# A four-layer block on one core, two lanes woven by tables of beats: one shared table per engine becomes one per lane

## The reference

```
x = x + jnp.tanh(g_xattn[0]) * _L0_xattn_ref(_layernorm(x, axis=-1), ctx_1024, ...)   # 16 heads of 8
x = x + jnp.tanh(g_ffn[0])   * _L0_ffn_ref(_layernorm(x, axis=-1), ...)    # 8 experts, top 2, plus shared
x = x + jnp.tanh(g_xattn[1]) * _L1_xattn_ref(...)                          # 16 heads of 8, biases
x = x + jnp.tanh(g_ffn[1])   * _L1_ffn_ref(...)    # self-attention, values and outputs by 8 experts a head
x = x + jnp.tanh(g_xattn[2]) * _L2_xattn_ref(...)                          # mLSTM, 4 heads
x = x + jnp.tanh(g_ffn[2])   * _L2_ffn_ref(...)                            # quantised, with a convolution
x = x + jnp.tanh(g_xattn[3]) * _L3_xattn_ref(...)                          # one wide head and an MLP
x = x + jnp.tanh(g_ffn[3])   * _L3_ffn_ref(...)                            # 16 experts, top 4, plus shared
```

```
v = jnp.einsum('bthe,bted->bhtd', mix_v, proj_v)
...
attn = jnp.einsum('bhij,bhjd->bihd', probs, v)
...
res = jnp.einsum('bthe,bthd,efd->bthf', mask_o, attn, Wo)
```

## Time and profile before

| | before |
|---|---|
| median of 3 runs (lowest to highest) | 2517.3 us (2514.52 to 2517.75) |
| the profiled execution's own time | 2514.25 us |
| its span, first to last instruction | 2512.2 us |
| busy: PE, DVE, ACT | 87%, 70%, 51% of the span |
| mean granted TensorE clock | 0.98 of full |
| DMA | 115.45 MB, mean 46 GB/s |

### The profile page before, as it was taken

One profiled execution on the slowest core, in us unless ns is written; L12 is line 12 of the kernel. 1 busy time (PEld: TensorE's weight loads), 2 busy tenths in 40 slices (PEclk: granted clock), 3 DMA queues, 4 the chain that ended last, 5 costly groups with the idle time before them and its releaser, 6 DMA issues.

```text
span 2512.2 us, 50619 instructions
## 1 busy us (share of the span) xinstructions
PE 2196.2 (87%) x19506; PEld 1569.4 (62%) x19506; DVE 1748.2 (70%) x5567; ACT 1282.0 (51%) x3714; POOL 141.0 (6%) x180
## 2 busy tenths in 40 slices
PE   7998889988899888998889988899888998899887
PEld 3667556675567755676556765557655576555765
DVE  6864777757777477774877757777487775777657
ACT  4365354654446544474444734447344473444734
POOL 0000100001000010000000011000110001100010
PEclk9999999999999999999999989999899998999999
DMA  4034000330004300042000520005100051000510
GB/s 168 1 92 96 17 5 1 99 88 18 5 1 105 82 17 5 1 117 70 18 5 1 134 53 20 3 1 139 48 20 3 1 139 48 20 3 8 145 35 5
DMA packets 312512, 115.45 MB, mean 46 GB/s; under 512 B 268752, under 2 KB 295376, under 8 KB 312016
## 3 DMA queue, kind: packets, MB, share of 16 engines
q1 hardware_dynamic: 312272, 112.23, 17.5%
HBM read 63.96 MB, written 48.23 MB: 45 GB/s over the span
## 4 chain that ended last, share of the span: by engine, by line
PE 43%; DVE 32%; DMA 8%; ACT 7%; issue 5%; POOL 4%; SPq 1%; DVEq 0%; ACTq 0%
PE banks L408 6%; PE banks L344 5%; ACT PP L820 4%; PE banks L463 3%; DVE nm L1160 3%; PE banks L547 3%; POOL mv L1699 2%; PE banks L341 2%; DMA va<-o_d 2%; DVE qk L1241 2%; PE banks L502 2%; PE banks L294 2%; DVE xn L1072 2%; PE banks L680 2%; DVE st L1065 2%
## 5 line engine op out<-in xcount | busy, mean ns | idle before, releaser
L820 ACT ACTIVATE PP<-banks,nm 128x128 f32<-128x128 f32 x1568 | 444.8, 396 | 220.7 <-DVE nm L1160 124.5
L1160 DVE TENSOR_REDUCE nm<-banks 128x4 f32<-128x512 f32 (+1 forms) x400 | 261.2, 675 | 177.7 <-PE banks L344 122.0
L408 PE MATMUL banks<-w_sb,PP 128*128 128x128 f32 x1536 | 247.1, 285 | 61.3 <-ACT PP L820 28.9
L294 PE MATMUL banks<-identb 128*128 128x256 bf16 x1408 | 237.5, 283 | 24.8 <-ACT PP L975 22.4
L408 PEld LDWEIGHTS banks<-w_sb,PP 128*128 128x128 f32 x1536 | 166.1, 142 | 148.0 <-issue 55.6
L1699 POOL TENSOR_TENSOR mv<-mv,half 128x2 f32<-128x2 f32 x160 | 112.8, 705 | 2197.9 <-DVE mv L1057 2197.9
L1203 DVE COPY PP<-banks 128x512 f32<-128x512 f32 x256 | 175.5, 690 | 63.5 <-PE banks L408 60.1
L463 PE MATMUL banks<-w_sb,qk 128*128 128x128 f32 x1280 | 178.0, 278 | 2.2 <-DVE qk L1304 1.3
L294 PEld LDWEIGHTS banks<-identb 128*128 128x128 bf16 x1408 | 135.6, 102 | 65.1 <-ACT PP L975 30.1
L463 PEld LDWEIGHTS banks<-w_sb,qk 128*128 128x128 f32 x1280 | 161.8, 192 | 18.7 <-issue 11.4
L811 ACT ACTIVATE xnT<-banks 128x256 f32<-128x256 f32 x128 | 49.2, 384 | 229.6 <-PE banks L302 229.6
(11 more groups left out here) (283 smaller groups left out, 4339.1 us busy)
## 6 DMA issues: line engine op xcount, KB each, us to landing
va<-v_d SPq DMA_DIRECT2D x32, 512.0 KB, 5.5
o_d<-oa SPq DMA_DIRECT2D x64, 256.0 KB, 3.5
va<-o_d SPq DMA_DIRECT2D x32, 512.0 KB, 4.4
pv_d<-PP SPq DMA_DIRECT2D x32, 256.0 KB, 3.5
oa<-pv_d SPq DMA_DIRECT2D x32, 256.0 KB, 3.1
v_d<-PP SPq DMA_DIRECT2D x16, 512.0 KB, 3.9
v_d<-tmp SPq DMA_DIRECT2D x16, 512.0 KB, 6.1
w_sb<-weights SPq DMA_DIRECT2D x1, 5599.0 KB, 23.5
```

Source lines behind the costliest of these rows:

```text
L294: pe.matmul(bank(k, n)[:, cols(c, T)], identb[:, :], bc(identb[:, :], 1, G), start=True, stop=True, skip_group_check=True)
L408: e = pe.transpose(bank(k, 2)[:, cols(j)], P[k][:, 512 * (u % 2) + 128 * j:][:, 0:128], ident)
L820: e = act.activation(P[k][:, 512 * (u % 2) + 128 * j:][:, 0:128], bank_[:, cols(j)], ACT.Exp, bias=nm[k][:, m:m + 1])
L1160: e = dve.tensor_reduce(m, b3(scores[:, 0:maps * 128], maps), AX.X, ALU.max, negate=True)
```

## The change

`SHIFT` is gone. Each engine's table becomes a pair, one table for each lane, and `SPARES` has new numbers.

```diff
@@ -92,7 +134,7 @@
     heads = []
     for k, lane in enumerate(lanes):
         next(lane)
-        heads.append([k * SHIFT + beats[0], k, 0, lane])
+        heads.append([beats[k][0], k, 0, lane])
...
-        turn, chunk = divmod(n + 1, len(beats))
-        head[0], head[2] = k * SHIFT + turn * TURN + beats[chunk], n + 1
+        turn, chunk = divmod(n + 1, len(beats[k]))
+        head[0], head[2] = turn * TURN + beats[k][chunk], n + 1
...
-TURN, SHIFT = 39873, 1339
-BEATS_PE = (
-    -2214, -466, -461, -93, 353, 697, 798, 1052, 1382, 1480, 1551, 1551, 1551, 1815, 2124, 2305, 2673, 2829, 3076, 3148,
+TURN = 39873
+BEATS_PE = ((
+    -1250, -612, -326, -44, 358, 653, 679, 1059, 1283, 1395, 1454, 1561, 1923, 2116, 2199, 2211, 2316, 2889, 2917, 2958,
```

More of the change, by code:

```diff
@@ L34 @@
 A0, M0, A1, SW, ML, CF, WA, M3 = range(8)
-TURN, SHIFT = 39873, 1339
-BEATS_PE = (
[11 rows of a table removed]
-BEATS_ACT = (
[7 rows of a table removed]
-BEATS_DVE = (
+TURN = 39873
+BEATS_PE = ((
[11 rows of a table added]
+), (
[11 rows of a table added]
+))
+BEATS_ACT = ((
[7 rows of a table added]
+), (
[7 rows of a table added]
+))
+BEATS_DVE = ((
     -19219, -10308, -5178, 370, 515, 809, 992, 1166, 1317, 1853, 1954, 1979, 2161, 2253, 2710, 3043, 3267, 3337, 3585, 4226,
@@ L67 @@
     31714, 31913, 34237, 34561, 35084, 35179, 35730, 35885, 36324, 36465, 36465, 36635, 36808, 36861, 37200, 37473, 37662,
[1 row of a table removed]
-BEATS_POOL = (
-    56292, 62108, 65236, 78903, 83359, 84939, 84939, 88197, 90116, 92203, 92980,)
-BEATS_SP = (
-    -178284, -178284, -178193, -178193, -177326, -177326, -177326, -177009, -177009, -176487, -175517, -168289, -168289,
-    -167984, -167955, -167955, -167775, -166618, -166580, -166580, -160674, -145843,)
[1 row of a table added]
+), (
[10 rows of a table added]
+))
+BEATS_POOL = ((
+    47832, 55688, 59143, 64674, 67070, 70207, 71015, 77823, 79861, 83113, 84484,
+), (
+    48901, 58347, 63494, 64749, 70006, 73170, 76144, 78979, 81361, 86183, 87523,
+))
+BEATS_SP = ((
+    -242752, -242553, -242553, -238131, -238131, -237804, -237804, -237058, -236981, -233923, -230618, -221598, -219346,
+    -218796, -217615, -212325, -212215, -209270, -206607, -206485, -203699, -203699,
+), (
+    -235003, -231213, -230164, -229008, -229008, -228143, -225901, -221262, -221262, -221262, -221262, -218853, -213790,
+    -209157, -209065, -206564, -205345, -205168, -204765, -204680, -203168, -203066,
+))
 SPARES = (
[3 rows of a table removed]
[3 rows of a table added]
+)
 XN_A0, XN_M0, XN_A1, XN_SW, XN_ML, XN_CF, XN_WA, XN_WA2, XN_M3 = range(9)
```

## The result

| | before | after |
|---|---|---|
| median (lowest to highest), 4 runs each on one chip | 2516.53 us (2514.52 to 2517.75) | 2449.92 us (2437.53 to 2453.32) |
| ratio, 95% interval | | 0.9727 (0.9691 to 0.9763) |
| the profiled execution: its time, span, granted clock | 2514.25, 2512.2, 0.980 | 2447.47, 2445.4, 0.976 |

The change takes 66.6 us off, 2.7%. The forecast said 2503, 0.6%, and its range ended at 2482.

The account below looks back on a forecast made before the run. No engine is full, so order and waits, with the switched attention's chain running through DMAs, were taken as the bound. Terms summed to -1.8 us a turn, eight times -14.4, giving a median of 2503 us (range 2482 to 2532).

Parts of the forecast that it names:

- Output stores: On SP, lane 0's third and fourth output stores go sooner, and its output projection follows: -2.0 us a turn (0 to -3.4).
- Gates of lane 1: Switched attention: lane 1's gate store waits behind lane 0's second store of mixed values: +1.2 us a turn (0 to +4.3).
- The sign to look for in the profile after: Lane 1's first gate load should land 1 to 2 us later against the turn's start.
- Lane 0's first exponentials and the copy on ACT: Exponentials could run some 5 us sooner, but PE's mixing still waits for lane 1's gates: worth 0.
- The other swaps: Neighbouring chunks on PE and ACT trade places, mostly putting the ready one first: -0.5 us a turn (-1.2 to +1.0).
- Spares: 54 more a turn on PE at 0.105 us each, mostly ahead of waits: +0.3 us a turn (0 to 5.7).
- Clock: Nine spares shorten idle time before the convolution, so four drops of 1.7 us go: -0.8 us a turn.
- The convolution's drop: Clock drop after lane 1's 2.34 us idle time, costing 1.7 us in four of eight turns, expected to go.
- the first rival: Lane 1's gate store loses more than the outputs gain, its term 4.3 instead of 1.2: 2528 us, chance 0.17.
- DVE didn't take it back: Rival: DVE, fixed order and 93% busy at the turn's end, absorbs the gain: no change, 2517 us, chance 0.16.
- the second rival: Half of the added spares' 5.7 us lie on the path, 2.9 instead of 0.3: 2524 us, chance 0.12.
- the clock stays up in most places: Rival: half of the 50 us lost at half clock come back thanks to more spares: 2485 us, chance 0.11.

Follow-up runs that it names:

- all_but_sp: The changed kernel with the old order on SP: 2449.51 us, ratio 0.9730 against the kernel before.
- only_sp: The kernel before with the new order on SP alone: 2520.31 us, ratio 1.0000.
- copy_order: The kernel before with lane 0's first copy of mixed values on ACT moved ahead of lane 1's three chunks: 2493.83 us, ratio 0.9925.
- early_order: The kernel before with new PE and ACT orders only in the two small attentions and the mixer between them, old spares: 2498.71 us, ratio 0.9924.
- order_min_tail: The kernel before with new PE and ACT orders, smaller of old and new spare counts through the mLSTM, new counts from the convolution on: 2463.17 us.
- min_to_mlstm: The kernel before with new PE and ACT orders, smaller of old and new spare counts ahead of the mLSTM, new counts from there: 2447.46 us.
- only_order: The kernel before with the new orders on PE and ACT alone, SP and spares old: 2484.34 us, ratio 0.9878.

## Why the prediction was wrong

By its own steps, in us a turn unless said otherwise:

- **Output stores, -2.0 (0 to -3.4).** Mechanism right. Lane 0's fourth store now starts 0.02 us after its outputs are ready (0.38 in one turn), and its second projection starts 4.9 us sooner against the start of the switched attention, where all_but_sp already has 3.8. Lane 0 gains 3.5 in the outputs' stage, lane 1 none.
- **Gates of lane 1, +1.2 (0 to +4.3).** Mechanism right, size 2.7 to 2.9. With the term above it comes to the measured zero of only_sp; the forecast had -0.8. The sign to look for in the profile after was wrong all the same: the load was to go later against the turn's start, and it leaves sooner, at 148.6 us in turn 3 where it was 152.8 (145.7 in all_but_sp), because the copy of the next term moved.
- **Lane 0's first exponentials and the copy on ACT, 0.** Failed. The forecast saw that the copy moves up and used this only to say when the store leaves. It took lane 1's gates as a fixed cover; the same copy's store was what held them. It is worth -2.4 to -2.8 (19 to 22 us in all, by copy_order's ratio and median).
- **The other swaps, -0.5 (-1.2 to +1.0).** Failed: -1.6 in the first attention and -1.4 in the mixer and the second, 19 us in all by early_order. The bound, one chunk of 0.5 to 1.2 us each way, was the wrong measure. The swap shown above is worth the wait of the chunk that is passed: it stands at the head of a chain of scores, maxima and exponentials. That the other swaps gain in the same way is read off the stage lengths, not shown one by one.
- **Spares, +0.3 (0 to 5.7).** Failed, and the step that missed by most: -4.4 with the new orders (35 us), +1.7 with the old. The price of one, 0.105 us, was right (0.109 from start to start at full clock in both traces, 0.213 at half). The sum was over 27 more a turn and lane, net; it was made of 79 added and 52 removed at other places, and only additions were priced, at places looked at in the old order. The chain's 2% of spares was on the page and wasn't read.
- **Clock, -0.8.** Failed. The convolution's drop did go, as forecast: lane 1's first stretch up to L722 takes the short time, 4.1 us, in all turns. But the time at half rose from 102 to 117 us, since what falls into lane 0's mLSTM rose from 46 to 89. By the Trainium skill (TensorE: Matmul & The Clock Gate, HAM oscillation) the penalty is the throttled time times one minus the share of the clock granted in it (one half here): 51 us before and 59 after, so by that rule alone the change would have lost 8 us through the clock. It holds between order_min_tail and min_to_mlstm (44 us less at half, 22 by the rule, 16 measured) and fails between before and only_order (51 us more at half, and 31 us faster), where the rest of the time moved too.

The rivals: the gates did lose more, as the first rival had it, but its 2528 left out that ACT's copy gave more back on the same path. DVE didn't take it back: its stage at the turn's end kept its length and moved as a whole, as the forecast argued. The spares did show, as the second rival had it, but only with the old orders. That the clock stays up in most places was no part of the gain: the time at half rose.

## What to carry to other kernels

Price a swap in a fixed order by the wait of what is passed and by what is queued behind it, on every queue that the moved instruction feeds, not by the length of the chunk. Where filler work changes, count additions and removals place by place, and read its share of the chain and the time at half clock together: filler laid out for one order lands on the path of another, and taking it out can cost more in clock than it gives. When a stage begins with filler, measure from the readiness of its operand, not from its first instruction.

## What the runs showed of the hardware

One ACT copy of 1.02 us moved past three chunks gave 0.75% of the run, since its DMA stood ahead of another lane's on SP. With nearly the same time at half clock (130 and 134 us) counts of 78 and 115 take the same time, and with 134 us at half 167 take 47 us more: the granted clock alone doesn't rank these kernels. And the same work of the mLSTM took 15.40 us at a granted 0.67 and 10.80 at 1.00, while in the window before it, with PE waiting, 14.00 us passed at 0.88 and at 0.76.
